# Wide-head attention with three-pass products, unrolled, in an eight-layer kernel on one NeuronCore

## Chip, cores and metric

The kernel runs on one core of one Trainium2 chip. The metric is the device time of one execution in microseconds, from which a run's time is taken; lower is better. PE is the engine of the matrix products, DVE the vector engine, ACT the scalar engine, POOL the GpSimd engine, SP the engine that issues most transfers.

## What is computed

Eight layers, each `x = x + layer(layernorm(x))`, on x of 32 sequences of 64 rows with 128 features (2048 rows, in 16 tiles of 128). The third layer is the one that changes:

```python
def _L1_xattn_ref(x, context, ln_gamma, ln_beta, w_q, w_kv, w_out, b_out, gate):
    xn = _layernorm(x, ln_gamma, ln_beta)
    q = (xn @ w_q).reshape(B, SQ, NUM_HEADS, DIM_HEAD)      # 16 heads of 64
    kv = context @ w_kv
    k, v = jnp.split(kv, 2, axis=-1)
    scores = jnp.einsum('bqhd,bkhd->bhqk', q * SCALE, k)
    attn = jax.nn.softmax(scores, axis=-1)
    out = jnp.einsum('bhqk,bkhd->bqhd', attn, v).reshape(B, SQ, INNER)
    out = out @ w_out + b_out
    return out * jnp.tanh(gate[0])
```

Its input is normalised twice, once by the residual step and once inside. The layer before it, F0, is a feed-forward layer (128 to 512 to 128, gelu); beside it the kernel already chooses the experts of a later mixture layer (E2) from the context alone.

## The kernel before

**Order.** Every engine runs one list of instructions, layer by layer; semaphores tie the lists together. An engine that waits holds up all that is behind it in its list. `experts` (L1214) writes the lists of F0, `wide_head_attention` (L864) those of the attention, `build` (L2712) what lies around them.

**Attention, per tile of 128 rows (two sequences).** The work of tile t is spread over five steps; step n handles tile n's norms and keys, n-1's rows and queries, n-2's scores and values, n-3's probabilities, n-4's output (L1037 to L1061). Steps 7 to 14 are a loop (`pipeline`, L48), the others are written out. On PE, in the order of a step: `scores` (L980), `turn_x` (L958, the normalised rows turned through the identity), `turn_probs` (L994), `queries` (L966), `turn_out` (L1020), `keys` (L933), `weigh_values` (L1006), `project` (L1031), `values` (L943). Queries, keys, values and the projection are float32 products.

Queries, keys, values and the turned rows share two PSUM banks, J0 and J1 (banks 0 and 1): whoever writes one waits until ACT or DVE has copied what was in it. Scores have two banks of their own, the turned probabilities, turned output and projection share two, the weighed values two.

ACT copies the turned rows with gamma and beta (L1075), the turned probabilities (L1083), queries (L1091), the turned output (L1099) and keys (L1107) out of PSUM and takes the exponentials (L1112). DVE does both norms (`Norm`, L125; each waits for POOL's power, L150), the maxima, subtraction, sums and division of the softmax, the gate and residual, and copies the values (L1197). POOL copies a piece of the context per tile for the value products (L1124).

**F0.** Its first products are already in three passes: a float32 operand is split into a high part in the format fp32r and the float32 rest, also kept in fp32r, and high x high, high x low and low x high are added up in PSUM (`product`, L1429):

```python
pe.matmul(out, WH[:, p, ws], XH[:, cols], start=True, stop=False)
pe.matmul(out, WH[:, p, ws], XL[:, cols], start=False, stop=False)
return pe.matmul(out, WL[:, p, ws], XH[:, cols], start=False, stop=True)
```

PE's list there: logits of the choice of experts (L1811), the turned norms (L234), first products of row groups 0 and 1, rank products (L1860), second products of group 0 (L1452), first of 2, second of 1, table products, first of 3, and so on. The rank products wait for DVE's `choose` (L1825): `take_best` twice (L1816: maximum, compare L1819, multiply L1821, maximum, compare L1823), then L1841 to L1844. POOL's list: the powers of the norms, the low parts of the rows (`low_part`, L245), then `owners` (L1614), which waits for DVE's places. DVE adds the second products to X, a row group at a time (L1719).

## Time and profile before

| | us |
|---|---|
| median of 3 runs | 964.1 (961.65 to 967.59) |
| profiled execution, span from first to last instruction | 1010.8 |
| profiled execution, what lies around the span | not recorded |
| busy in the span: PE / DVE / ACT / POOL | 783.2 / 608.2 / 486.4 / 372.9 |
| wide-head attention on PE, from / to | 147.6 / 343.8 |

The profiled execution is longer than the runs; its rows are used for durations and differences. Times in rows are microseconds from the start of the span unless marked ns. A float32 product shows as two records on PE, a product in fp32r as one; a record lasts longer than the distance to the next, since matmuls are pipelined, so distances are read from starts. "PEclk" is the granted clock of PE as a share of 2.4 GHz.

### The profile page before, as it was taken

The page shows a single profiled execution, that of the slowest core. Times are in us where ns is not written, and L with a number is a line of the kernel's source. Part 1 is how long each engine was busy: PE and PEld are TensorE (multiplying, and loading weights), DVE is VectorE, ACT ScalarE, POOL GpSimd, SP SyncE. Part 2 cuts the span into 40 slices and gives each one's busy share as a digit, 9 for nine tenths or more (in the row PEclk, how much of TensorE's full clock was granted, in tenths as well). Part 3 has the DMA queues.
Part 4 walks back from the last instruction along what each step waited for, and adds up shares of the span by engine and source line. Part 5 has one row for each costly group of instructions (what it writes and reads, how often), then busy time and mean ns, then how long its engine had stood idle before and what let it go on. Part 6 is the DMA issues. An engine that isn't in the chain of part 4 may idle for free.

```text
span 1010.8 us, 24129 instructions
## 1 busy us (share of the span) xinstructions
PE 783.2 (77%) x8041; PEld 646.4 (64%) x8041; DVE 608.2 (60%) x1568; ACT 486.4 (48%) x984; POOL 372.9 (37%) x492
## 2 busy tenths in 40 slices
PE   6998899999999789996477775667677559969005
PEld 3766787888888679985476664667676526644005
DVE  3886747777777667767353224632222368867895
ACT  3886434555444344432154435334444357745753
POOL 5663421111111331111566653155556535550810
PEclk9999699999999979999699989579989769978557
DMA  6300000000000000033332213101111300000001
GB/s 187 96 0 1 1 1 3 2 3 0 0 0 3 1 11 19 21 102 103 95 100 88 64 41 105 42 19 43 40 37 45 85 23 3 0 1 1 0 0 42
DMA packets 49218, 36.06 MB, mean 36 GB/s; under 512 B 7665, under 2 KB 44978, under 8 KB 49138
## 3 DMA queue, kind: packets, MB, share of 16 engines
q1 hardware_dynamic: 43420, 24.45, 8.5%
q0 software_dynamic: 4992, 10.23, 3.6%
q8 instruction: 48, 0.79, 0.3%
q10 hardware_dynamic: 726, 0.33, 0.1%
q14 instruction: 32, 0.26, 0.1%
HBM read 26.73 MB, written 8.26 MB: 35 GB/s over the span
## 4 chain that ended last, share of the span: by engine, by line
PE 67%; DVE 9%; another core or an unknown queue 6%; issue 5%; ACT 5%; DMA 3%; DVEq 2%; POOL 2%; ACTq 1%; SPq 1%; POOLq 0%
PE psum L2118 9%; PE psum L1464 7%; PE psum L2143 4%; PE psum L1034 3%; PE psum L976 3%; PE psum L954 3%; PE psum L939 3%; PE psum L2442 2%; PE psum L1431 2%; PE psum L1432 2%; PE psum L1433 2%; PE psum L323 2%; PE psum L1016 2%; PE psum L663 2%
## 5 line engine op out<-in xcount | busy, mean ns | idle before, releaser
L2118 PE MATMUL psum<-E_XT,E_weights 128*128 128x128 f32 x780 | 114.3, 298 | 52.4 <-ACT E_XT L2198 27.7
L2118 PEld LDWEIGHTS psum<-E_XT,E_weights 128*128 128x128 f32 x780 | 103.0, 209 | 61.2 <-ACT E_XT L2198 30.8
L2266 POOL DMA_INDIRECT y_scratch<-E_y,route_place_of x78 | 78.8, 1010 | 83.2 <-DVE E_y L2321 37.8
L2258 POOL DMA_INDIRECT E_rows<-rows_scratch,route_token_of x78 | 76.4, 979 | 32.1 <-issue 25.5
L1723 DVE SCALAR_TENSOR_TENSOR X<-psum,E_gates,X 128x128 f32<-128x128 f32 x256 | 71.7, 344 | 26.5 <-PE psum L1464 26.4
L1464 PEld LDWEIGHTS psum<-E_w,E_h 128*128 128x128 f32 x512 | 69.4, 198 | 11.5 <-issue 3.5
L2221 ACT ACTIVATE E_h<-psum,cols 128x128 f32<-128x128 f32 x156 | 44.5, 368 | 66.4 <-issue 31.3
L1548 ACT ACTIVATE E_h<-psum,cols 128x512 f32<-128x512 f32 x64 | 43.8, 687 | 67.8 <-PE psum L1433 67.7
L1464 PE MATMUL psum<-E_w,E_h 128*128 128x128 f32 x512 | 70.4, 282 | 4.8 <-DVE X L1723 3.8
L2311 DVE TENSOR_TENSOR E_h<-E_sg,psum 128x384 f32<-128x384 f32 x39 | 21.6, 554 | 77.5 <-remote 26.8
L203 POOL TENSOR_TENSOR rstd<-vareps,nhalf 128x4 f32<-128x4 f32 x24 | 24.6, 1029 | 75.0 <-DVE vareps L197 74.9
L235 PE MATMUL psum<-ident,xn 128*128 128x128 f32 x80 | 20.0, 400 | 35.9 <-ACT xn L226 24.5
L2143 PE MATMUL psum<-L1w,E_h 128*128 x312 | 44.4, 288 | 0.5 <-DVE E_y L2323 0.5
L150 POOL TENSOR_TENSOR A_A_inner_rstd<-A_A_inner_vareps,nhalf 128x1 f32<-128x1 f32 x16 | 8.7, 543 | 95.5 <-DVE A_A_inner_vareps L144 95.5
L788 POOL TENSOR_TENSOR A_kexp<-E_first,hmask 128x512 f32<-128x512 f32 x32 | 32.7, 1042 | 30.0 <-PE psum L663 29.9
L2431 PE MATMUL psum<-ident,Q_amax_rows 128*1 128x128 f32 x5 | 1.7, 332 | 52.1 <-DVE Q_amax_rows L2539 51.4
L235 PEld LDWEIGHTS psum<-ident,xn 128*128 128x128 f32 x80 | 14.0, 210 | 43.5 <-issue 21.5
L2323 DVE TENSOR_TENSOR E_y<-psum,E2b2all 128x128 f32<-128x128 f32 x39 | 11.3, 290 | 49.6 <-PE psum L2143 27.9
L2143 PEld LDWEIGHTS psum<-L1w,E_h 128*128 128x128 f32 x312 | 40.4, 202 | 1.0 <-issue 0.7
L2114 PE MATMUL psum<-ident,E_rows 128*128 128x128 f32 x78 | 22.8, 293 | 22.3 <-DMA E_rows<-rows_scratch,route_token_of 22.3
L2204 ACT ACTIVATE E_weights<-E_first 128x768 f32 x39 | 32.9, 843 | 14.2 <-issue 13.9
L1075 ACT ACTIVATE A_xnT<-psum,cols 128x128 f32<-128x128 f32 x16 | 7.3, 457 | 65.3 <-PE psum L964 65.3
(346 smaller groups left out, 2160.2 us busy)
## 6 DMA issues: line engine op xcount, KB each, us to landing
routed_back<-y_scratch SPq DMA_DIRECT2D x16, 256.0 KB, 4.9
E_first<-in_L_xattn_W SPq DMA_DIRECT2D x1, 2048.0 KB, 8.6
L1w<-in_L_xattn_W SPq DMA_DIRECT2D x8, 256.0 KB, 4.7
rows_scratch<-xn SPq DMA_DIRECT2D x8, 256.0 KB, 2.3
E_w<-in_L_ffn_routed_w SPq DMA_DIRECT2D x28, 64.0 KB, 1.9
E_raw<-in_L_ffn_w_down SPq DMA_DIRECT2D x8, 176.0 KB
E_rows<-rows_scratch,route_token_of POOLq DMA_INDIRECT x78
y_scratch<-E_y,route_place_of POOLq DMA_INDIRECT x78
```

The costliest lines, as they stand in the source:

```text
L235: tr = pe.transpose(self.bank[:, i * P:(i + 1) * P], self.m.xn[:, g * GT + i, :], self.m.ident[:, :])
L788: ke = pool.tensor_tensor(kexp[:, p, b], kk.broadcast_to([P, HP, S]), m.hmask[:, :].rearrange("p (h o) -> p h o", o=1).broadcast_to([P, HP ...
L939: mm = pe.matmul((J1, J0)[j][:, c * P:(c + 1) * P], w["k"][:, cc * P:(cc + 1) * P], columns(m.ctxT, t, P), start=True, stop=True)
L1464: mm = pe.matmul(y_bank(e, g)[:, i * P:(i + 1) * P], h[:, g % 2, c, i * P:(i + 1) * P], w2[:, p, c, :], start=(c == 0 and i == 0), stop=(c ...
L1548: act.activation(h[:, g % 2, c, :], ring[(C * g + c) % 4], spec["func"], bias=spec["b1"][:, bass.ds(e * C + c, 1)]).then_inc(h_ready.sem, 1)
L1723: st = dve.scalar_tensor_tensor(out=m.X[:, t, :], in0=y_bank(e, g)[:, i * P:(i + 1) * P], scalar=gates[:, t, bass.ds(e, 1)], in1=m.X[:, t, :],
L2118: mm = pe.matmul(out[:, c * P:(c + 1) * P], WE[:, p, (k0 + c) * P:(k0 + c + 1) * P], XT[:, p, :], start=True, stop=True)
L2143: mm = pe.matmul(Y[p][:, 0:P], h[:, p, c, :], W2[:, bass.ds(e, 1), c, :].rearrange("p o d -> p (o d)"), start=c == 0, stop=c == C - 1)
L2204: act.activation(WE[:, i % 2, :], W1[:, bass.ds(e, 1), :].rearrange("p o f -> p (o f)"), ACT.Copy).then_inc(w_ready.sem, 1)
L2221: ac = act.activation(h[:, p, c, :], m.banks[2 + i % 3][:, c * P:(c + 1) * P], spec["func"], bias=spec["b1"][:, bass.ds(e * C + c, 1)])
L2258: pool.indirect_dma_start(out=xg[:, i % 4, :], out_offset=None, in_=rows[:, :], in_offset=bass.IndirectOffsetOnAxis(ap=disp.token_of[:, i: ...
L2266: pool.indirect_dma_start(out=yrows[:, :], in_=y[:, i % 3, :], in_offset=None, out_offset=bass.IndirectOffsetOnAxis(ap=disp.place_of[:, i: ...
```

## The change

- Queries, keys and values are computed in three passes in fp32r instead of float32. Weights: ACT makes the high parts of the three matrices before F0 (`wide_high`), POOL the low parts inside F0, ahead of `owners` (`low_parts`). Context: ACT copies four high pieces and POOL subtracts four low ones at the start of the attention. Rows: ACT copies the turned rows twice (high part, full), POOL subtracts.
- Queries and keys are computed for a pair of tiles (256 columns) and half of the heads at a time, one such half per step. Values are one bank per half of the heads' dimension order; DVE copies those of even heads, ACT those of odd heads, two copies of 64 partitions each.
- The work of a tile spreads over seven steps; all are written out, no loop is left.
- On PE `turn_x` stands behind `turn_probs`, then keys, turned output, queries.
- The norms of tiles 0 and 1 are done by DVE in F0, ahead of the last two additions to X; two pairs' keys and one pair's queries stand in the lists ahead of the wait for F0's end.

The diff, cut:

```diff
+    xH, xL = (m.split_rows[:, i, :].rearrange("p (r q) -> p r q", q=PW) for i in range(2))
+    CH, CL = m.split
+    WH, WL = m.wide_high, m.wide_low
...
+        def three(out, wk, cc, xs, start=True):
+            ws = slice(cc * P, (cc + 1) * P)
+            pe.matmul(out, WH[:, wk, ws], xs[0], start=True, stop=False)
+            pe.matmul(out, WH[:, wk, ws], xs[1], start=False, stop=False)
+            return pe.matmul(out, WL[:, wk, ws], xs[0], start=False, stop=True)
...
+        def keys(i, free):
+            pair, half = i // 2, i % 2
+            cols = slice(pair * PW, (pair + 1) * PW)
+            pe.wait_ge(*ctx_low(pair // 2 + 1))
             for j in range(2):
...
+                if free[j]:
+                    pe.wait_ge(*free[j])
+                for c in range(2):
+                    mm = three((J1, J0)[j][:, c * PW:(c + 1) * PW], 1, 4 * half + 2 * j + c, (CH[:, cols], CL[:, cols]))
                 mm.then_inc(k_ps.sem, 1)
...
+        def turn_x(t, free):
+            pe.wait_ge(*xn_ready(t + 1))
+            if free:
+                pe.wait_ge(*free)
+            pe.transpose(J0[:, 0:P], xn[:, t % 2, :], m.ident[:, :]).then_inc(xnT_ps.sem, 1)
+        def queries(i, free):
...
+            pe.wait_ge(*x_low(2 * pair + 2))
+            for j in range(2):
+                pe.wait_ge(*free[j])
+                for c in range(2):
+                    mm = three((J1, J0)[j][:, c * PW:(c + 1) * PW], 0, 4 * half + 2 * j + c, (xH[:, r, :], xL[:, r, :]))
+                mm.then_inc(q_ps.sem, 1)
...
+                if n <= NT + 1:
+                    pe.wait_ge(*q_ready(2 * (n - 2) + u + 1))
                 else:
...
+                    pe.wait_ge(*(v_even, v_odd)[u](t))
+                bank = (J1, J0)[u]
+                pe.matmul(bank, CH[:, cols], wv[0][:, :, u, :], start=True, stop=False)
+                pe.matmul(bank, CL[:, cols], wv[0][:, :, u, :], start=False, stop=False)
+                mm = pe.matmul(bank, CH[:, cols], wv[1][:, :, u, :], start=False, stop=True)
                 mm.then_inc(v_ps.sem, 1)
...
+        turn_x(0, None)
+        keys(0, (None, xnT_ready(1)))
+        turn_x(1, k_ready(2))
+        keys(1, (k_ready(1), xnT_ready(2)))
+        queries(0, (k_ready(3), k_ready(4)))
+        queries(1, (q_ready(1), q_ready(2)))
+        keys(2, (q_ready(3), q_ready(4)))
+        keys(3, (k_ready(5), k_ready(6)))
+        m.begin(pe, start)
         def step(n, p):
             q = 1 - p
...
+            if is_tile(n - 4):
+                scores(n - 4)
+            if is_tile(n - 5):
+                turn_probs(n - 5, q)
+            if n >= 3 and is_tile(n - 1):
+                turn_x(n - 1, v_odd(n - 4) if n >= 5 else xnT_ready(3) if n == 4 else k_ready(8))
+            if after(tag) and n == NT + 4:
+                pe.wait_ge(*v_odd(NT))
+                after(tag).turn(pe, 0)
+            if 5 <= n <= NT:
+                keys(n - 1, (v_even(n - 4), xnT_ready(n)))
+            if is_tile(n - 6):
+                turn_out(n - 6, p)
+            if n == 4:
+                queries(2, (k_ready(7), xnT_ready(4)))
+            elif 5 <= n <= NT:
+                queries(n - 2, (k_ready(2 * n - 1), k_ready(2 * n)))
+            elif n == NT + 1:
+                queries(n - 2, (v_even(n - 4), v_odd(n - 4)))
+            if is_tile(n - 5):
+                weigh_values(n - 5, q)
+            if after(tag) and n == NT + 5:
+                after(tag).turn(pe, 1)
+            if is_tile(n - 6):
+                project(n - 6, p)
+            if is_tile(n - 4):
+                values(n - 4, n)
...
+        for g in range(NG):
+            cols = slice(g * GW, (g + 1) * GW)
+            act.activation(CH[:, cols], m.ctxT[:, cols], ACT.Copy).then_inc(ctx_high.sem, 1)
+        def keys_kept(i):
+            pair, half = i // 2, i % 2
+            if pair >= 2:
+                act.wait_ge(*scores_ready(2 * pair - 2))
+            for j in range(2):
+                c = 4 * half + 2 * j
+                act.wait_ge(*k_ps(2 * i + j + 1))
+                act.activation(kT[pair % 2][:, c:c + 2, :].rearrange("p c k -> p (c k)"), (J1, J0)[j],
+                               ACT.Copy).then_inc(k_ready.sem, 1)
+        def rows_kept(t):
...
+            act.activation(xH[:, t // 2 % 2, t % 2 * P:(t % 2 + 1) * P], J0[:, 0:P], ACT.Identity, bias=w["beta"],
+                           scale=w["gamma"])
+            if t >= 2:
+                act.wait_ge(*x_low(t - 1))
+            act.activation(xnT[:, t % 2, :], J0[:, 0:P], ACT.Identity, bias=w["beta"],
+                           scale=w["gamma"]).then_inc(xnT_ready.sem, 1)
+        def queries_kept(i):
+            pair, half = i // 2, i % 2
+            if pair >= 2:
+                act.wait_ge(*scores_ready(2 * pair - 2))
+            for j in range(2):
+                c = 4 * half + 2 * j
+                act.wait_ge(*q_ps(2 * i + j + 1))
+                act.activation(qT[pair % 2][:, c:c + 2, :].rearrange("p c q -> p (c q)"), (J1, J0)[j],
+                               ACT.Copy).then_inc(q_ready.sem, 1)
...
+            if is_tile(n - 5):
+                t = n - 5
+                if t >= 2:
                     act.wait_ge(*o_ps(t - 1))
                 for half in range(2):
                     act.wait_ge(*probT_ps(2 * t + half + 1))
                     act.activation(probT[:, q, 4 * half:4 * half + 4, :].rearrange("p c q -> p (c q)"),
                                    pP[:, half, :], ACT.Copy).then_inc(probT_ready.sem, 1)
...
+            if n >= 3 and is_tile(n - 1):
+                rows_kept(n - 1)
+            if 5 <= n <= NT:
+                keys_kept(n - 1)
+            if is_tile(n - 6):
+                t = n - 6
+                if t >= 2:
                     act.wait_ge(*out_ps(t - 1))
                 for j in range(2):
                     act.wait_ge(*oT_ps(2 * t + j + 1))
                     act.activation(oT[:, p, 4 * j:4 * j + 4, :].rearrange("p c q -> p (c q)"), pP[:, j, :],
                                    ACT.Copy).then_inc(oT_ready.sem, 1)
...
+            if n >= 4 and is_tile(n - 2):
+                queries_kept(n - 2)
+            if is_tile(n - 4):
+                act.wait_ge(*sub_ready(n - 3))
                 pr = prob[:, p].rearrange("p h k -> p (h k)")
                 act.activation(pr, pr, ACT.Exp, scale=scale).then_inc(prob_ready.sem, 1)
...
+                act.wait_ge(*v_ps(2 * n - 6))
+                if n >= 6:
+                    act.wait_ge(*o_ps(n - 5))
+                for b in range(2):
+                    cp = act.activation(v[S:P, p, b].rearrange("p c d -> p (c d)"), J0[b * S:(b + 1) * S, :], ACT.Copy)
+                cp.then_inc(v_odd.sem, 1)
...
+        for t in range(2):
+            outer.rstd(pool, t, t, x1_ready)
+            inner.rstd(pool, t, t, xn_ready)
+        for g in range(NG):
+            cols = slice(g * GW, (g + 1) * GW)
+            pool.wait_ge(*ctx_high(g + 1))
+            pool.tensor_tensor(CL[:, cols], m.ctxT[:, cols], CH[:, cols], ALU.subtract).then_inc(ctx_low.sem, 1)
...
+            pool.tensor_tensor(xL[:, t // 2 % 2, at], xnT[:, t % 2, :], xH[:, t // 2 % 2, at],
+                               ALU.subtract).then_inc(x_low.sem, 1)
+        low_part(0)
+        low_part(1)
         m.begin(pool, start)
...
+    def early_rows(dve, t):
+        outer.stats(dve, tile_of(m.X, t), t, t)
+        outer.apply(dve, x1[:, t, :], tile_of(m.X, t), t, t).then_inc(x1_ready.sem, 1)
+        dve.wait_ge(*x1_ready(t + 1))
+        inner.stats(dve, x1[:, t, :], t, t)
+        inner.apply(dve, xn[:, t, :], x1[:, t, :], t, t).then_inc(xn_ready.sem, 1)
...
+                dve.wait_ge(*v_ps(2 * t + 1))
                 for b in range(2):
...
+                    cp = dve.tensor_copy(v[0:S, p, b].rearrange("p c d -> p (c d)"), J1[b * S:(b + 1) * S, :])
+                cp.then_inc(v_even.sem, 1)
...
+            spec["pool_between"](pool)
             for j in range(NCH):
                 beside.owners(pool, j)
...
+                if beside and g >= 2:
+                    dve.wait_ge(*combined(1))
+                    m.early_rows(dve, g - 2)
                 dve.wait_ge(*y_ps(u + 1))
...
+        def low_parts(pool):
+            for i, k in enumerate((1, 0, 2)):
+                pool.wait_ge(wide_high_ready, i + 1)
+                pool.tensor_tensor(m.wide_low[:, k, :], wide[:, k, :], m.wide_high[:, k, :], ALU.subtract
+                                   ).then_inc(wide_low_ready, 1)
...
+            for k in (1, 0, 2):
+                act.activation(m.wide_high[:, k, :], wide[:, k, :], ACT.Copy).then_inc(wide_high_ready, 1)
             for L in layers[1:]:
                 L.scalar(act)
```

## Rows read from the trace of the kernel before

**Rows 1.** Windows: us, length, busy PE, PEld, DVE, ACT, POOL, PEclk, DMA.

```profile
240.00:270.00 30.00, 30.00 (x539) 24.65 (x529) 22.58 (x47) 13.25 (x24) 2.83 (x7) 1.00 0.00 0
147.60:343.80 196.20, 189.53 (x3226) 159.24 (x3227) 148.87 (x318) 95.08 (x164) 27.74 (x54) 1.00 0.01 2
```

**Rows 2.** Chain that ended last, one tile of the attention: start us, us, what.

```profile
232.68 1.09 PE psum L990 x64
234.03 0.87 PE psum L1001 x8
234.90 1.89 PE psum L976 x16
236.79 0.87 PE psum L1027 x8
237.66 1.79 PE psum L939 x16
239.45 1.09 PE psum L1016 x64
240.54 1.98 PE psum L1034 x16
242.53 1.87 PE psum L954 x8
244.39 1.09 PE psum L990 x64
```

**Rows 3.** Chain that ended last, in F0: one fp32r pass of 512 columns, 16 of 40.

```profile
123.27 0.23 PE psum L1433
...
134.08 1.70 PE psum L1930 x16
```

**Rows 4.** Timeline of the attention: start us, us, engine, line, operation [idle before].

```profile
245.41 0.33 PE L964 MATMUL psum<-ident,A_xn 128*128 128x128 f32 x1
...
245.58 1.04 PE L1001 MATMUL psum<-ident,A_prob 128*128 128x128 f32 x8
...
245.86 0.46 ACT L1075 ACTIVATE A_xnT<-psum,cols 128x128 f32<-128x128 f32 x1 [4.83 <-PE psum L964]
...
246.22 1.08 ACT L1083 ACTIVATE A_probT<-psum 128x512 f32<-128x512 f32 x2
...
246.45 2.04 PE L976 MATMUL psum<-A_xnT,L1w 128*128 128x128 f32 x16
```

**Rows 5.** Timeline of F0.

```profile
108.78 0.60 ACT L242 ACTIVATE F_XH<-psum 128x512 fp32r<-128x512 f32 x1 [8.10 <-PE psum L235]
...
114.65 1.28 POOL L249 TENSOR_TENSOR F_XL<-XNT,F_XH 128x512 fp32r<-128x512 f32 x1 [1.09 <-ACT XNT L243]
...
115.09 0.98 DVE L1819 TENSOR_TENSOR route_work<-route_logits,route_best 128x128 f32<-128x128 f32 x1
...
117.00 1.27 POOL L249 TENSOR_TENSOR F_XL<-XNT,F_XH 128x512 fp32r<-128x512 f32 x1 [1.08 <-ACT XNT L243]
...
118.78 0.29 DVE L1819 TENSOR_TENSOR route_work<-route_at,route_best 128x128 f32<-128x128 f32 x1
...
120.96 0.29 DVE L1844 TENSOR_TENSOR route_ahead<-route_upto,route_both 128x128 f32<-128x128 f32 x1
...
123.34 0.38 PE L1865 MATMUL psum<-route_both,earlier 128*128 128x128 f32 x2
...
147.62 0.69 DVE L1719 TENSOR_TENSOR X<-X,psum 128x512 f32<-128x512 f32 x1 [4.67 <-PE psum L1464]
```

**Rows 6.** Timeline of the layer behind the attention.

```profile
356.69 5.38 POOL L1607 TENSOR_SCALAR E_b2sel<-L1b2rep,tmask 128x128 f32<-128x128 f32 x8
...
358.72 0.39 DVE L1638 TENSOR_TENSOR E_work<-E_work,E_row 128x224 f32<-128x224 f32 x1
```

**Rows 7.** Windows behind a pause of PE, columns as in rows 1.

```profile
597.34:601.29 3.95, 0.01 (x1) 0.00 (x0) 0.72 (x2) 0.27 (x1) 1.95 (x2) 1.00 0.34 49
601.70:605.10 3.40, 3.40 (x18) 3.40 (x17) 1.01 (x3) 1.60 (x6) 1.95 (x2) 0.50 0.07 24
```

More of the change, by code:

```diff
@@ L919, in wide_head_attention, with steps, is_tile @@
     L.done = x_done(NT)
[L920 to L927 removed]
+    END = NT + 7
+    first_products_done = m.split_free
+    after = m.stats_after.get
+    def steps(step):
+        for n in range(2, END):
+            step(n, n % 2)
+    def is_tile(t):
+        return 0 <= t < NT
     def tensor(pe):
[L930 removed]
         pe.wait_ge(*m.dispatch.owner_ready(1))
[L933 to L983 removed]
@@ L984, in scores @@
+        def scores(t):
+            a, r = t % 2, t // 2 % 2
+            pe.wait_ge(*q_ready(4 * (t // 2) + 4))
+            pe.wait_ge(*k_ready(4 * (t // 2) + 4))
+            if t >= 1:
                 pe.wait_ge(*sub_ready(t))
@@ new lines, in step @@
+            if after(tag) and n == NT + 5:
[4 more added lines that the diff above has]
+                values(n - 4, n)
+        steps(step)
+    def scalar(act):
+        for s, n in first_products_done:
+            act.wait_ge(s, n)
+        for g in range(NG):
[11 more added lines that the diff above has]
+        def rows_kept(t):
+            act.wait_ge(*xnT_ps(t + 1))
+            if t >= 4:
+                act.wait_ge(*q_ps(4 * (t // 2) - 4))
+            act.activation(xH[:, t // 2 % 2, t % 2 * P:(t % 2 + 1) * P], J0[:, 0:P], ACT.Identity, bias=w["beta"],
[5 more added lines that the diff above has]
+        def queries_kept(i):
+            pair, half = i // 2, i % 2
+            if pair >= 2:
[5 more added lines that the diff above has]
+                               ACT.Copy).then_inc(q_ready.sem, 1)
+        rows_kept(0)
+        keys_kept(0)
+        rows_kept(1)
+        keys_kept(1)
+        queries_kept(0)
+        queries_kept(1)
+        keys_kept(2)
+        keys_kept(3)
@@ new lines, in step, with low_part @@
+            if after(tag) and NT + 4 <= n < NT + 6:
+                after(tag).evacuate(act, n - NT - 4)
+        steps(step)
+    def gpsimd(pool):
+        for t in range(2):
[5 more added lines that the diff above has]
+            pool.tensor_tensor(CL[:, cols], m.ctxT[:, cols], CH[:, cols], ALU.subtract).then_inc(ctx_low.sem, 1)
+        def low_part(t):
+            at = slice(t % 2 * P, (t % 2 + 1) * P)
+            pool.wait_ge(*xnT_ready(t + 1))
+            pool.tensor_tensor(xL[:, t // 2 % 2, at], xnT[:, t % 2, :], xH[:, t // 2 % 2, at],
+                               ALU.subtract).then_inc(x_low.sem, 1)
+        low_part(0)
+        low_part(1)
@@ L1119, in gpsimd @@
         m.begin(pool, start)
-        def context(t, p):
-            if past(t, 2):
-                pool.wait_ge(*v_ps(2 * t - 2))
-            pool.tensor_copy(ctx1[:, p, :], columns(m.ctxT, t, P)).then_inc(ctx1_ready.sem, 1)
+        outer.rstd(pool, 2, 0, x1_ready)
         def step(n, p):
-            if live(n):
+            if is_tile(n):
                 inner.rstd(pool, n, p, xn_ready)
-            if live(n + 1):
+            if n >= 3 and is_tile(n - 1):
+                low_part(n - 1)
+            if is_tile(n + 1):
@@ L1130, in step @@
                 outer.rstd(pool, n + 1, 1 - p, x1_ready)
-            if live(n - 1):
-                context(n - 1, 1 - p)
-        outer.rstd(pool, 0, 0, x1_ready)
-        pipeline(pool, step, LO, HI, END)
-        if begun(NT):
+        steps(step)
+        if after(tag):
             for g in range(NG - 1):
-                follower().rstd(pool, g)
+                after(tag).rstd(pool, g)
             for g in range(2):
-                follower().low_part(pool, g)
-                follower().residual(pool, g)
+                after(tag).low_part(pool, g)
+                after(tag).residual(pool, g)
@@ L2787, in build @@
         b0["o"] = spread("L0bo", ins["L0_xattn_bo"], load_first)
+        with ExitStack() as early:
+            m.wide_low = early.enter_context(nc.sbuf_tensor("L1w_low", [P, 3, 1024], F32R))
         wide = sb("L1w", [P, 4, 1024])
```

221 lines of the change are left out of this document (65 added, 156 removed).

## Prediction

> **What bounds the kernel now.** I read the busy windows first. The wide-head attention fills the stretch from 147.6 to 343.8 us, 196.2 us, with PE busy for 189.5 of them at granted clock 1.00, the 2.4 GHz level; inside it PE is busy for all 30.00 us from 240 to 270, while DVE has 22.58 and ACT 13.25 [rows 1]. The chain of waits then says what PE does there: one tile lasts 244.39 - 232.68 = 11.71 us and every piece is PE's, end to end [rows 2]. In order: scores 1.09 (and 0.26 up to the next piece, in which the rows of the next tile are turned), probabilities turned 0.87, queries 1.89, output turned 0.87, keys 1.79, values weighed 1.09, projection 1.98, values 1.87. So a microsecond taken from PE in a tile shortens the tile by as much, until PE has to wait for something.
>
> **Sum against which time.** The durations come from a profiled execution with a span of 1010.8 us, 46.7 above the median of 964.1 us of the runs. What I find is a difference inside the span, and I subtract it from the median unchanged; the stage concerned waits on no DMA.
>
> **Products in three passes.** Queries and keys are now 12 passes of 256 columns per tile each (24 per pair of tiles), values 6 of 512. A pass over 512 columns in the same format takes 0.23 us, one over 40 takes 1.70/16 = 0.106 [rows 3]. For 256 no row exists: below, 0.106; above, the straight line between the two, 0.163. I take half of the 512-column pass, 0.115, because the long pass is the nearer in that it streams columns for most of its time. Then queries cost 12 x 0.115 = 1.38 instead of 1.89, keys 1.38 instead of 1.79, values 6 x 0.23 = 1.38 instead of 1.87: 1.41 us less per tile, 16 x 1.41 = 22.6 us of PE time.
>
> **The rows turned behind the probabilities.** This gives much of it back. In a step PE now does: probabilities turned, rows turned (bank 0), first half of the keys (bank 1), second half of the keys (bank 0). The second half waits until ACT has emptied bank 0, and ACT's list in that step begins with the two copies of the turned probabilities, then two copies of the rows (high part and full) where there was one. From the start of the turned probabilities: ACT's first copy starts at 0.64 (245.58 to 246.22), the two take 1.08, so the rows start at 1.72; the first row copy lets the next start 0.36 later (245.86 to 246.22), the second takes 0.46, done at 2.54; PE follows 0.13 later (246.32 to 246.45), at 2.67 [rows 4]. PE itself was ready at 0.87 + 0.17 + 6 x 0.115 = 1.73. It stands for 0.94 us, in each of the 12 steps that have keys: 11.3 us. Bounds: 0, if ACT could copy the rows first, which its order forbids; 1.1 with passes of 0.106, since PE then only waits longer. The new steady tile is 11.71 - 1.41 + 0.94 = 11.24 us.
>
> What else waits in the step is covered. The turned rows need the odd values copied by ACT: about 0.2 + 2 x 0.6 = 1.4 us after the values, against 1.96 of scores and probabilities; cover gone, 1.4 would stand there. The even values keep DVE's two copies; DVE needs 22.58/30 x 11.71 = 8.8 us per tile, below 11.24. ACT rises from 5.2 by two copies and a row copy (1.6) to 6.8. Unrolling takes away loop bookkeeping that the chain doesn't show; I cost it at nothing, bounds 0.1 us per tile either way.
>
> **Filling and draining.** Before: 196.2 - 16 x 11.71 = 8.8 us in which no tile advances. Now four key products and two query products stand ahead, on two banks that ACT empties between uses. A half lasts 0.69, its copy is seen by PE after about 0.2 (the 0.64 above less half of 0.87) + 0.6 + 0.13 = 0.93, a turned tile of rows after 0.17 + 0.2 + 0.82 + 0.13 less the half behind which it hides, 0.5. The first two key products cost 0.5 + 0.93 + 0.5, the next four calls 0.24 each (0.69 + 0.93 for a bank against 1.38 of work), the last copy 0.93: 3.8 us. In the step of the first scores the third pair's queries wait for two tiles' rows one after the other and POOL's low part: about 3.4. With 5 for the drain, 12.2 to 13 instead of 8.8: +4.0. Bounds 0 and +8.
>
> Attention: -22.6 + 11.3 + 4.0 = -7.3 us.
>
> **Work put into the layer before.** ACT's three high parts of the weights (128x1024 each, twice the 0.60 copy, about 3.3 together) fall into its 8.10 us of idleness before 108.78; the first norms of two tiles fall into DVE's waits ahead of its last two additions to X, the last 4.67 [rows 5]. Both nothing; without the cover 3.3 and 3.8.
>
> POOL's three low parts are another matter. They follow POOL's last subtraction, which ends at 118.27, and POOL's next work is far off, so POOL's own time is free. But POOL's subtraction holds up DVE: an operation of DVE on two SBUF operands that met one took 0.98 us and ended 0.14 after POOL, alone it took 0.29 [rows 5]. The three new ones run just while DVE picks the two best experts, the chain from 118.78 to 121.25 on which PE's rank products wait. PE came to these at 123.34, 2.1 us later [rows 5]. Each new subtraction has 1024 columns, at most twice 1.27: 2.5 us. In turn with DVE: POOL to 120.8, best-of compare 120.95, POOL to 123.45, next multiply 123.6, POOL to 126.1, next compare 126.25, and the half of the chain that is left, 1.2 us: 127.45. PE stands for 4.2 us instead of nothing. If POOL went through first, 118.3 + 7.5 + 2.5 = 128.3: 5.0. The floor is 0, if DVE isn't held.
>
> A pause of that length also costs clock: after PE's pause of 3.95 us from 597.34 the granted clock was 0.50, the 1.2 GHz level, for the next 3.4 us of full work [rows 7]: 1.7 us lost. The layer before: 4.2 + 1.7 = +5.9, bounds 0 and 7.
>
> The Trainium skill's page "SBUF — State Buffer", section "SBUF: two separate sides", has VectorE and GpSimd share one pair of ports as a lock held for a whole instruction, against VectorE operations with two SBUF inputs. By it the wait is certain and the sum is the one I make, 962.7. The trace agrees for subtractions, but not for every POOL operation that reads SBUF: while POOL's multiplies by a column ran, DVE's two-operand compare took its plain 0.39 us [rows 6]; by those rows the sum would be 956.8.
>
> **Sum:** -7.3 + 5.9 = -1.4 us; 964.1 - 1.4 = 962.7 us.
>
> **Rivals.**
> *The low parts hold nobody up.* For it: rows 6. Against: the slowed compare in rows 5, same kind of POOL operation. Only the attention counts: 964.1 - 7.3 = 956.8 us. Chance 0.20.
> *The second half of the keys doesn't wait.* If ACT's copies overlap more than the rows show, the 11.3 us stay gained: 962.7 - 11.3 = 951.4. Against: four copies in a row on one engine. Chance 0.13.
> *The 256-column pass costs more than half the long one* (the slower side). Loading 128 columns of weights may set the pace, as it seems to with 40 columns at 0.106. 24 passes x 16 tiles less the 72 hidden in the wait are 312; each 0.01 us costs 3.1 us. From 0.12 on the kernel is slower than before; at 0.163 it is 962.7 + 312 x 0.048 = 977.7. Against: 512 columns at 0.23 leave little for the load. Chance 0.13.
> *The early keys don't come early,* because the low parts of the context on POOL come late: then the filling costs its bound, +4, 966.7. I keep it within the forecast's range.
>
> **How the numbers follow.** Forecast 0.54, its own range 958 to 968. One per cent, 9.6 us, is about what a measurement of this kernel can tell from no change. Faster by more: most of the second rival (0.12), a tail of the first (0.05) and of the forecast (0.02): 0.19. Slower by more: most of the pass rival (0.09) and a tail (0.02): 0.11. Within: 0.70. The range 950 to 972 takes in the first two rivals and the cheaper half of the third.
>
> **What would show it.** In the profile after: steady scores 11.1 to 11.4 us apart, with 0.9 us of idleness in the middle of the keys released by ACT's second row copy; 256-column passes at 0.115; DVE's compares stretched to over 2 us beside POOL's low parts, PE idle some 4 us ahead of the rank products, clock 0.50 after it; first scores about 12.5 us after the last product of the layer before. The forecast is wrong if the keys run without a gap, if the rank products start at 123.3 as before, or if a pass takes 0.13 or more.

## The result and the profile after

The changed kernel takes 966.8 us (median of 15 runs) against 961.8 us for the kernel before in the same measurement. The two medians lie 5.0 us apart; the ratio taken over all runs is smaller, 1.0034, interval 1.0019 to 1.0049, which is 3.3 us slower. The forecast was 1.4 us faster. A second measurement, beside the experiments, gave 1.0015 (0.9997 to 1.0034); the two intervals overlap.

The profiled execution after has a span of 965.1 us. The one before had 1010.8, but that difference lies behind the stretch compared here, in the later mixture layers, which the change does not touch. So I compare one stretch of the two traces: from F0's first product to the router's products behind the attention. It lasts from 115.45 to 344.08 before, 228.63 us, and from 115.31 to 346.97 after, 231.66 us: 3.03 more, close to the 3.3 of the ratio. It splits like this. F0 ends where its last product ends: before at 147.6 as in [rows 1] (the attention's first PE instruction starts at 148.36, after a wait of 0.78 us for DVE), after at 152.49, where the attention's first PE instruction follows at once. A step is counted from one tile's scores to the next tile's.

| stretch | before | after | difference |
|---|---|---|---|
| F0, from its first product to the end of its last | 32.15 | 37.18 | +5.03 |
| to the first scores | 9.28 | 12.76 | +3.48 |
| first scores to third scores | 16.55 | 18.61 | +2.06 |
| third scores to fourteenth (11 steps) | 129.42 | 124.70 | -4.72 |
| fourteenth scores to the router's products | 41.23 | 38.41 | -2.82 |

The busy windows of the kernel after, over the same marks (columns as in rows 1; the third window is the first of the two first steps alone):

```profile
115.30:152.50 37.20, 33.81 (x217) 30.88 (x215) 29.74 (x56) 16.53 (x26) 16.98 (x14) 0.89 0.00 1
152.50:165.25 12.75, 11.08 (x78) 9.48 (x76) 6.00 (x26) 9.06 (x17) 6.79 (x10) 1.00 0.00 1
165.25:174.98 9.73, 6.81 (x84) 5.51 (x84) 5.43 (x13) 3.75 (x7) 2.46 (x5) 0.65 0.01 3
183.86:308.56 124.70, 117.30 (x2103) 106.19 (x2102) 95.30 (x187) 78.86 (x143) 15.34 (x30) 1.00 0.01 3
308.56:346.97 38.41, 33.95 (x644) 29.97 (x643) 31.05 (x66) 20.59 (x35) 6.84 (x7) 1.00 0.01 2
```

PE, which stands for 0.87 of the 129.42 us of the steady stretch before, now stands for 7.40 of 124.70; and in the step of the first scores, 9.73 us, it is busy for 6.81 of them at a mean granted clock of 0.65.

**F0.** POOL's three low parts and DVE's choice of the second expert, in the timeline of the kernel after:

```profile
118.09 7.20 POOL L2944 TENSOR_TENSOR L1w_low<-L1w,L1w_high 128x1024 fp32r<-128x1024 f32 x3
...
118.31 0.28 DVE L1898 TENSOR_REDUCE route_best<-route_at 128x16 f32<-128x128 f32 x1
118.64 2.04 DVE L1899 TENSOR_TENSOR route_work<-route_at,route_best 128x128 f32<-128x128 f32 x1
120.71 2.38 DVE L1901 TENSOR_TENSOR route_work<-route_work,rev 128x128 f32<-128x128 f32 x1
123.12 0.29 DVE L1902 TENSOR_REDUCE route_rowmax<-route_work 128x16 f32<-128x128 f32 x1
123.44 2.00 DVE L1903 TENSOR_TENSOR route_second<-route_work,route_rowmax 128x128 f32<-128x128 f32 x1
...
126.71 0.49 PE L1945 MATMUL psum<-route_both,earlier 128*128 128x128 f32 x2 [3.39 <-DVE route_ahead L1924]
```

The compare that took 0.29 [rows 5] takes 2.04, and the two operations behind it 2.38 and 2.00: each ends when a low part ends. PE reaches the rank products at 126.71 instead of 123.34. From 127.06 to 130.48 the granted clock is 0.50. Six further traces have the same F0 (e0, e2, e3, e4, e9 and e10 below): the rank products come 11.39 to 11.41 us after the first product in each, PE stands for 3.46 to 4.46 us ahead of them, and F0 takes 37.17 to 38.18 us. A difference of less than 1 us in F0 between two traces therefore says little.

**A steady tile.** The chain of waits after, from one tile's scores to the next (rows to hold against [rows 2]):

```profile
240.59 1.09 PE psum L996 x64
241.68 0.60 PE psum L1007 x4
...
242.36 0.40 ACT A_probT L1142
...
242.85 0.59 ACT A_probT L1142
243.45 0.12 ACT A_xnT_split L1107
...
243.67 0.48 ACT A_xnT L1111
...
244.20 0.39 PE psum L940
244.58 0.12 PE psum L941
...
245.17 0.87 PE psum L1034 x8
246.05 0.12 PE psum L940
...
247.46 1.09 PE psum L1023 x64
248.55 1.98 PE psum L1041 x16
250.53 0.23 PE psum L980
...
251.93 0.20 PE psum L996
```

251.93 - 240.59 = 11.34 us. The chain leaves PE after the first half of the turned probabilities, runs through ACT's two copies of probabilities and two of rows, and comes back with the second half of the keys (L940 at 244.20). The timeline shows the gap: the first half's last pass starts at 243.24, and the second half at 244.20.

```profile
243.24 0.28 PE L942 MATMUL psum<-E_XH,L1w_low 128*128 128x256 f32 x1
244.20 0.39 PE L940 MATMUL psum<-E_XH,L1w_high 128*128 128x256 f32 x1 [0.68 <-ACT A_xnT L1111]
```

Less one pass of 0.12 that is 0.84 us. The product groups are as short as forecast: queries 246.05 to 247.46, 1.41; values 250.53 to 251.93, 1.40.

**The step of the first scores.** Timeline of PE and POOL there:

```profile
165.25 1.16 PE L996 MATMUL psum<-XNT,xn 64*64 64x64 f32 x64
166.40 0.30 PE L959 MATMUL psum<-ident,A_xn 128*128 128x128 f32 x1
169.61 0.58 PE L940 MATMUL psum<-A_xnT_split,L1w_high 128*128 128x256 f32 x1 [2.92 <-POOL A_xnT_split L1185]
...
172.34 0.63 PE L980 MATMUL psum<-L1w_high,E_XH 128*128 128x512 f32 x1
...
168.59 0.54 POOL L150 TENSOR_TENSOR A_A_inner_rstd<-A_A_inner_vareps,nhalf 128x1 f32<-128x1 f32 x1 [1.31 <-DVE A_A_inner_vareps L144]
169.11 0.45 POOL L1185 TENSOR_TENSOR A_xnT_split<-A_xnT,A_xnT_split 128x128 fp32r<-128x128 f32 x1
```

PE waits 2.92 us for POOL's low part of the fourth tile's rows; POOL makes it only after the inner norm of the fifth tile, for which it waits for DVE. The granted clock is 0.50 from 168.02 to 174.85, so that 12 passes of queries take 172.34 - 169.61 = 2.73 us (1.59 in the steady tile, also from start to start) and the values 174.98 - 172.34 = 2.64 (1.57).

**The end.** In the last three steps with scores there are no keys between the turned probabilities and the turned output; the two share PSUM banks. PE stands for 0.89 us in each of the three (at 311.63, 321.61 and 330.15). The kernel before, whose queries stand between the two, shows that wait in one step only, the last with scores. Timeline after, then before:

```profile
328.17 1.09 PE L1007 MATMUL psum<-ident,A_prob 128*128 128x128 f32 x8
330.15 1.06 PE L1034 MATMUL psum<-ident,A_on 128*128 128x128 f32 x8 [0.89 <-ACT A_probT L1142]
```

```profile
327.36 1.06 PE L1027 MATMUL psum<-ident,A_on 128*128 128x128 f32 x8 [0.89 <-ACT A_probT L1083]
```

### The profile page after: what moved, and what is told of

The parts are those of the page before. It is cut to its first block, busy times and chain, and to the rows that moved or that the text cites. A ratio compares the mean times of both kernels' runs of the same rounds, so it can differ in the third digit from the quotient of the medians.

```text
span 965.1 us, 23563 instructions
## 1 busy us (share of the span) xinstructions
PE 766.1 (79%) x7881; PEld 638.3 (66%) x7881; DVE 615.3 (64%) x1568; ACT 515.5 (53%) x1039; POOL 389.6 (40%) x499
## 4 chain that ended last, share of the span: by engine, by line
PE 60%; DVE 9%; POOL 9%; issue 8%; ACT 7%; DMA 5%; SPq 1%; ACTq 1%; DVEq 0%; POOLq 0%
PE psum L1540 7%; PE psum L2198 5%; PE psum L2223 4%; PE psum L1041 3%; POOL y_scratch L2346 3%; POOL E_rows L2338 3%; PE psum L2522 2%; DMA E_rows<-rows_scratch,route_token_of 2%; PE psum L323 2%; PE psum L1023 2%; PE psum L1507 2%; PE psum L1509 2%; ACT A_probT L1142 2%; PE psum L996 2%; PE psum L1508 2%
## 5 line engine op out<-in xcount | busy, mean ns | idle before, releaser
L2198 PE MATMUL psum<-E_XT,E_weights 128*128 128x128 f32 x780 | 104.2, 282 | 1.5 <-DVE E_XT L2376 0.8
L2198 PEld LDWEIGHTS psum<-E_XT,E_weights 128*128 128x128 f32 x780 | 97.2, 199 | 2.7 <-DVE E_XT L2376 1.5
L1166 ACT ACTIVATE A_v<-psum 64x512 f32<-64x512 f32 x32 | 18.9, 591 | 42.9 <-PE psum L982 42.7
L1655 POOL CAST E_WH<-E_w 128x128 fp32r<-128x128 f32 x16 | 4.6, 290 | 91.7 <-DMA E_w<-in_L_ffn_routed_w 72.5
```

The costliest lines, as they stand in the source:

```text
L2198: mm = pe.matmul(out[:, c * P:(c + 1) * P], WE[:, p, (k0 + c) * P:(k0 + c + 1) * P], XT[:, p, :], start=True, stop=True)
```

## The experiments

All start from the changed kernel. The stretches are read from each run's trace as in the table above; "first step" is from the first scores to the second, "whole" from F0's first product to the router's products.

| run | F0 | to first scores | first step | steady tile | whole | ratio to the kernel before |
|---|---|---|---|---|---|---|
| changed | 37.18 | 12.76 | 9.73 | 11.34 | 231.66 | 1.0034 (1.0019 to 1.0049) |
| changed, again (e0) | 37.79 | 12.75 | 9.78 | 11.34 | 232.34 | 1.0015 (0.9997 to 1.0034) |
| low parts apart (e1) | 32.04 | 12.76 | 8.90 | 11.34 | 225.67 | 0.9968 (0.9954 to 0.9982) |
| rows first (e2) | 37.20 | 12.75 | 9.78 | 10.73 | 224.93 | 0.9946 (0.9924 to 0.9967) |
| low part before norm (e3) | 37.62 | 12.75 | 7.41 | 11.34 | 229.76 | 0.9988 (0.9966 to 1.0010) |
| third pair early (e4) | 38.18 | 14.05 | 4.85 | 11.34 | 229.06 | 0.9980 (0.9958 to 1.0002) |
| e1, e2 and e4 (e5) | 31.66 | 14.05 | 4.84 | 10.73 | 215.58 | 0.9889 (0.9861 to 0.9917) |
| and the drain (e6) | 31.98 | 14.03 | 4.86 | 10.73 | 214.93 | 0.9867 (0.9848 to 0.9887) |
| one operand (e7) | 31.94 | 12.74 | 9.48 | 11.34 | 226.14 | one run, 960.6 us |
| norm order only (e8) | 35.13 | 12.75 | 8.89 | 11.34 | 228.75 | one run, 961.0 us |
| busy wait (e9) | 37.17 | 12.74 | 7.63 | 11.34 | 229.53 | 1.0008 (0.9989 to 1.0026) |
| fourth pass (e10) | 37.20 | 14.35 | 9.86 | 12.53 | 249.27 | one run, 979.8 us |

The ratios differ by up to 0.0024 from what the whole stretch says, in either direction (e0: 3.71 us more than before would be 1.0038, the ratio is 1.0015; e5: 13.05 less would be 0.9865, the ratio is 0.9889); the rest of the kernel, with lower-clock stretches of its own, is in the ratio too. Where a part is at issue I go by the stretch.

> The changed kernel once more, beside the others on one chip. It stands to the kernel before as it did: 1.0019 to 1.0049. If it comes out nearer to 1, the runs with one edit owe as much of their gain to the chip.

It came out at 1.0015, somewhat nearer to 1, so up to 0.002 of the gains in ratio may be the chip's. Its steps, 9.78 and 11.34, are those of the first trace; F0, 37.79, is 0.6 longer.

### F0: the low parts' place, their operands, the norm's order

```diff
+        norm.rstd(pool, 3)
+        between = spec.get("pool_between")
+        for g in range(2 if begun else 0, NG):
+            if between and g < 3:
+                between(pool, g)
+            norm.low_part(pool, g)
...
-            spec["pool_between"](pool)
             for j in range(NCH):
```

> Against the changed kernel (966.8 us). Only where POOL makes the three low parts of the weights changes: one ahead of each of its first three low parts of the rows, around 108 to 117 us, instead of all three behind the last one. Theory that the subtractions hold up DVE's expert-choosing chain: DVE's compares of the second choice are back at 0.3 to 1.2 us each, PE comes to the rank products at 123.3 to 124.5 instead of 126.71, the stretch at granted clock 0.50 behind them is gone, the attention's first PE instruction is at 147.5 to 148.7 instead of 152.49: 4 to 5 us less, 962 to 963, ratio to the kernel before 1.000 to 1.001. Rival, that PE's late rank products have another cause (DVE's order, the clock): 966.8, ratio 1.0034 to 1.005.

F0 took 32.04 us, 5.1 less, with PE busy in all of it and no lower clock behind the rank products, which came 7.96 us after the first product instead of 11.40. The whole stretch is 6.0 shorter, more than expected: the other 0.8 are in the step of the first scores, where PE waits 2.92 us as before but the granted clock is 0.50 for only 3.4 us.

```profile
118.08:150.12 32.04, 32.04 (x216) 29.36 (x215) 25.73 (x56) 16.58 (x26) 12.06 (x12) 0.92 0.00 1
```

But the edit does two things: the low parts move, and POOL's last power of the norms moves ahead of its first low part of the rows. So two further runs. The first leaves the place as it was and puts a multiplication by a column where the subtraction was. It reads one large operand instead of two, and the low parts themselves are left out:

```diff
-                pool.tensor_tensor(m.wide_low[:, k, :], wide[:, k, :], m.wide_high[:, k, :], ALU.subtract
+                pool.tensor_scalar(m.wide_low[:, k, :], wide[:, k, :], tmask16[:, 0:1], None, ALU.mult
```

> The weights' three low parts are left out: in their place, in the same place of POOL's list, stand three multiplications by a column, 128x1024 each, one large SBUF operand instead of two. Theory that it is the second operand (two reads of SBUF) that holds up DVE, as the multiplications in the kernel before's trace did not: DVE's second-choice compares take 0.3 to 0.5 us, rank products 8 us after the first product, no stretch at granted clock 0.50 behind them. Rival, that any POOL instruction that works on SBUF for so long holds DVE: compares of 1.5 to 2.5 us, rank products 11.4 us after the first product, as in the changed kernel.

Timeline of that run, the same operations of DVE beside POOL's multiplications (the third follows at once; the three take 9.22 us, longer than the subtractions' 7.20):

```profile
119.89 5.81 POOL L2944 TENSOR_SCALAR L1w_low<-L1w,tmask 128x1024 fp32r<-128x1024 f32 x2
...
120.41 0.77 DVE L1899 TENSOR_TENSOR route_work<-route_at,route_best 128x128 f32<-128x128 f32 x1
121.22 0.29 DVE L1901 TENSOR_TENSOR route_work<-route_work,rev 128x128 f32<-128x128 f32 x1
121.54 0.29 DVE L1902 TENSOR_REDUCE route_rowmax<-route_work 128x16 f32<-128x128 f32 x1
121.86 0.29 DVE L1903 TENSOR_TENSOR route_second<-route_work,route_rowmax 128x128 f32<-128x128 f32 x1
```

2.04, 2.38 and 2.00 us have become 0.77, 0.29 and 0.29, F0 takes 31.94 us, and nothing else was changed. It is POOL's two-operand subtraction that holds DVE; a longer instruction with one large operand holds it much less (one later operation, `route_ahead`, took 1.02 instead of 0.29). The edit changes the operation together with the number of operands, so that the second operand is the cause, and not the subtraction as such, is not shown.

The second does the norm's order alone:

```diff
-        if not begun:
-            norm.low_part(pool, 0)
         norm.rstd(pool, 3)
-        for g in range(2 if begun else 1, NG):
+        for g in range(2 if begun else 0, NG):
             norm.low_part(pool, g)
```

> Control for the run with the low parts apart, which also put POOL's last rstd ahead of its first low part of the rows: only that is done here, the weights' low parts stay behind the others. Theory (the place of the low parts did it): rank products 11.4 us after the layer's first product, as in the changed kernel. Rival (the earlier norm did it): about 8.

Here the rival was right about the rank products: they came 7.83 us after the first product. The earlier power lets DVE finish its norms and its choice by 116.89, before the low parts start at 117.98. F0 still took 35.13 us, because the hold now falls on what DVE does next:

```profile
123.93 0.94 DVE L1955 TENSOR_SCALAR route_ntile<-route_ntile 128x8 f32<-128x8 f32 x1
124.90 2.29 DVE L1956 TENSOR_TENSOR_SCAN route_ntile<-ones,route_ntile 128x8 f32<-128x8 f32 x1
...
134.60 1.07 PE L2008 MATMUL psum<-route_A,route_B 128*128 128x40 f32 x8 [0.96 <-POOL route_A L2000]
```

A scan over 8 columns takes 2.29 us (0.17 in the kernel after), the places come late, and PE stands for 0.96 us ahead of the table products, with the granted clock at 0.50 from 136.95 to 140.36. So of e1's 5.1 us the earlier norm alone gives 37.18 - 35.13 = 2.05, and with it in place the low parts' new place gives 35.13 - 32.04 = 3.1. These are single traces; F0 of the changed kernel alone differs by up to 1.0 us between traces.

### The steady tile: rows first

PE's list, then ACT's:

```diff
+            if n >= 3 and is_tile(n - 1):
+                turn_x(n - 1, v_odd(n - 4) if n >= 5 else xnT_ready(3) if n == 4 else k_ready(8))
             if is_tile(n - 5):
                 turn_probs(n - 5, q)
-            if n >= 3 and is_tile(n - 1):
-                turn_x(n - 1, v_odd(n - 4) if n >= 5 else xnT_ready(3) if n == 4 else k_ready(8))
```

```diff
+            if n >= 3 and is_tile(n - 1):
+                rows_kept(n - 1)
             if is_tile(n - 5):
...
-            if n >= 3 and is_tile(n - 1):
-                rows_kept(n - 1)
```

> Against the changed kernel (966.8 us). Rows are turned ahead of the probabilities, and ACT copies them ahead of the probabilities. Theory that the second half of the keys stands for ACT's row copies, 0.93 us in each of 12 steps: the gap in the keys is gone, PE waits 0.15 to 0.3 for the odd values ahead of the turned rows instead, the steady tile falls from 11.34 to 10.6 to 10.75, 12 x 0.6 to 0.75 = 7 to 9 us less: 958 to 960, ratio 0.996 to 0.998. Rival, that the wait for the odd values or the now later copies of the probabilities takes as much as the gap gave: tile 11.2 to 11.4, 965 to 967, ratio 1.002 to 1.004.

The tile fell to 10.73 us. The gap in the keys is gone, and PE waits 0.28 us for the odd values instead; the timeline of that run:

```profile
261.20 0.30 PE L959 MATMUL psum<-ident,A_xn 128*128 128x128 f32 x1 [0.28 <-ACT A_v L1166]
261.34 1.05 PE L1007 MATMUL psum<-ident,A_prob 128*128 128x128 f32 x8
...
263.65 1.03 PE L1034 MATMUL psum<-ident,A_on 128*128 128x128 f32 x8
```

From the turned probabilities to the turned output it is 2.31 us (261.34 to 263.65) where it was 3.40 (241.61 to 245.01, in the timeline of the changed kernel). The whole stretch is 6.7 us shorter, a little less than the 7 to 9 expected: 6.4 in the eleven steady steps and 0.4 in the second step.

The opposite probe adds work:

```diff
-            return pe.matmul(out, WL[:, wk, ws], xs[0], start=False, stop=True)
+            pe.matmul(out, WL[:, wk, ws], xs[0], start=False, stop=False)
+            return pe.matmul(out, WL[:, wk, ws], xs[1], start=False, stop=True)
```

(and the same in the values)

> The changed kernel with a fourth pass in each product of queries, keys and values (low part by low part): 4 passes of 256 columns more in queries, 4 in keys, 2 of 512 in values. By 0.117 and 0.235 a pass, with the two in the first half of the keys hidden in the wait for ACT's copies: 6 x 0.117 + 2 x 0.235 = 1.17 us more, a steady tile of 12.5 us with the gap in the keys down from 0.93 to 0.70; the last product of the attention some 18 us later. Rival, that PE isn't the bound or that the wait grows with the work: tile under 12.2, or 12.75 and more with the gap as it was.

The tile is 12.53 us. Six passes of 0.117 and two of 0.235 add 1.17, 1.19 were measured; the two passes in the first half of the keys cost nothing. The gap, read as above, shrank from 244.20 - 243.24 - 0.12 = 0.84 to 251.05 - 250.33 - 0.12 = 0.60, by just those two passes:

```profile
250.33 0.28 PE L943 MATMUL psum<-E_XL,L1w_low 128*128 128x256 f32 x1
251.05 0.39 PE L940 MATMUL psum<-E_XH,L1w_high 128*128 128x256 f32 x1 [0.44 <-ACT A_xnT L1113]
```

### The step of the first scores

```diff
+            if n == 4:
+                low_part(n - 1)
             if is_tile(n):
                 inner.rstd(pool, n, p, xn_ready)
-            if n >= 3 and is_tile(n - 1):
+            if (n == 3 or n >= 5) and is_tile(n - 1):
                 low_part(n - 1)
```

> Against the changed kernel (966.8 us). In the step of the first scores POOL makes the low part of the fourth tile's rows ahead of the inner norm of the fifth tile, instead of behind it; nothing else. Theory that the order on POOL holds up the third pair's queries: they start at 168.1 to 168.3 instead of 169.61, 1.4 us less, and as much as 2.2 more where PE's shorter pause keeps the granted clock at 1.00: 963.2 to 965.4, ratio 1.0015 to 1.0037. Rival, that ACT's copies or DVE's norm set the time of the queries: they start at 169.6, 966.8.

The step took 7.41 us, 2.3 less. The queries started 2.87 us after the first scores instead of 4.36, the 1.5 us that the theory said: the order on POOL was holding them up. The clock did not stay at 1.00, though; it was 0.50 for 3.4 us (168.97 to 172.39) instead of 6.8, which gives the other 0.8. The whole stretch is 1.9 shorter, with F0 0.4 longer.

The next run has the same order on POOL, and turns the third tile's rows between the early keys, the fourth's ahead of the first scores:

```diff
         keys(2, (q_ready(3), q_ready(4)))
-        keys(3, (k_ready(5), k_ready(6)))
+        turn_x(2, k_ready(6))
+        keys(3, (k_ready(5), xnT_ready(3)))
...
+            if n == 3:
+                turn_x(3, k_ready(8))
```

(and the same order of copies on ACT)

> Against the changed kernel (966.8 us). As the run with the low part ahead of the norm, and besides the rows of the third tile are turned and copied between the early keys of the third pair, those of the fourth ahead of the first scores. Theory that the lateness of the rows makes the step of the first scores long: the third pair's queries start at 166.4 to 167 instead of 169.61, 2.6 to 3.2 us less, and the granted clock stays at 1.00 through that step, 2.2 us more: from first scores to second scores 5 to 5.5 us instead of 9.73 if all goes well, and 961.5 to 963, ratio 0.9997 to 1.001. Rival, that the clock falls all the same, since it fell before the queries' wait had ended: 963.6 to 964.2, ratio 1.002. Rival, that the time comes back in the next step: no change.

The step took 4.85 us. The stretch to the first scores grew by 1.3, which the expectation had left out, so together 18.90 instead of 22.49. PE's wait and the windows of the step (columns as in rows 1):

```profile
173.82 0.38 PE L940 MATMUL psum<-A_xnT_split,L1w_high 128*128 128x256 f32 x1 [0.42 <-POOL A_xnT_split L1191]
```

```profile
172.23:177.08 4.85, 4.43 (x84) 3.48 (x83) 3.54 (x9) 2.95 (x5) 0.95 (x2) 1.00 0.01 3
```

The granted clock is 1.00 throughout. Whether that is because the pause is shorter could still be chance, so the next run keeps the pause and fills it:

```diff
             if n == 4:
+                pe.wait_ge(*k_ready(7))
+                for i in range(8):
+                    three(J1[:, i % 2 * PW:(i % 2 + 1) * PW], 1, 0, (CH[:, 0:PW], CL[:, 0:PW]))
                 queries(2, (k_ready(7), xnT_ready(4)))
```

> The changed kernel with 24 more passes of 256 columns on PE ahead of the third pair's queries, 24 x 0.117 = 2.8 us of work whose result is written over, in the time in which PE waits for the rows. Nothing else moves. Theory that 2.2 us of the step of the first scores are the lower clock alone: the granted clock stays at 1.00 through the step, queries take 1.4 to 1.6 us and values 1.5 to 1.6 as in the steady tiles, and the step from first to second scores is 7.4 to 7.7 us instead of 9.73 in spite of the added work; 2 us less in all. Rival, that the queries and values of that step are slow for another reason, or that the added work is not hidden: 9.5 to 10.5 us.

With 24 useless passes the step is 2.1 us shorter, 7.63 instead of 9.73, and its clock is 1.00, although the queries start as late as before, 4.38 us after the first scores (4.36 in the changed kernel; columns as in rows 1):

```profile
163.37:171.00 7.63, 7.53 (x108) 6.42 (x107) 4.95 (x13) 3.76 (x7) 2.47 (x5) 1.00 0.01 3
```

So 2.1 of the 9.73 us are the lower clock and nothing else. The price is not the same in every trace: with a wait of 2.9 us each, the step took 9.78 us in e0 and e2, 9.48 in e7, but 8.90 and 8.89 in e1 and e8, where the clock was 0.50 for 3.4 us instead of 6.8. Against 7.63 that is 1.3 to 2.2 us.

### All together, and the end

> The three edits that each helped, together: the weights' low parts apart, rows turned and copied ahead of the probabilities, the third pair's rows early. Theory that they act on three stretches that don't overlap: against the changed kernel 5.1 us less in the layer before, 12 x 0.61 = 7.3 in the steady tiles, 3.6 in the first steps, 16.0 together: from the first product of the layer before to the router products behind the attention 231.66 - 16.0 = 215.7 us, some 948 to 951 in all, ratio to the kernel before 0.986 to 0.989. Rival, that they share what they gain (PE waiting for the context's low parts or for the first norms where the layer before ends earlier): 10 to 13 less, ratio 0.989 to 0.992.

The whole stretch took 215.58 us, 16.1 less than the changed kernel's: the three parts add up. The run takes 951.9 us, ratio 0.9889.

```diff
+            if n >= NT + 2 and is_tile(n - 4):
+                values(n - 4, n)
             if after(tag) and n == NT + 4:
...
-            if is_tile(n - 4):
+            if n < NT + 2 and is_tile(n - 4):
                 values(n - 4, n)
```

> As the run with all three edits, and besides in the last two steps that have scores the values' products stand ahead of the turned output instead of at the step's end. Theory that PE's two waits of 0.89 us for ACT's copies of the probabilities, which the keys cover in the steady steps, come from nothing but the missing work: they are gone, 1.8 us less than the run with all three, the last scores 7.6 to 7.7 us after those before instead of 8.53. Rival, that the values now wait 0.3 to 0.5 each for the copies of those before and the copies come late for the products that weigh them: 0 to 0.8 less.

Scores to scores fell from 8.53 to 7.45 us, a little more than the theory said, but the step behind gained nothing: PE now reaches the last turned probabilities before DVE has read the projection from the same bank. The timeline of that run:

```profile
322.64 1.06 PE L1007 MATMUL psum<-ident,A_prob 128*128 128x128 f32 x8 [1.38 <-DVE A_tmp L1267]
```

From the fourteenth scores to the router's products it is 37.50 us instead of 38.41, so 0.91 of the 1.8 us are left; the whole stretch shows 0.65 because F0 came out 0.32 longer. The first of the three waits, at the fourteenth scores, stays. It is the fastest version of this study, 951.7 us and 0.9867 of the kernel before; its lead over the run without the last edit is within the intervals.

## Why the prediction was wrong

**The step that failed** is "Filling and draining", in the sum as +4.0 us with bounds 0 and +8. The attention was forecast at 7.3 us less and came out at 3.48 + 2.06 - 4.72 - 2.82 = -2.0; 5.3 us are missing. With the products' -22.6 and the gaps' +11.3 as they stand in the sum, that leaves +9.3 for filling and draining, or about +8.2 without what belongs to the steady tile: twice the forecast, at its upper bound. Where it went:

- The clock in the step of the first scores, 2.1 (busy wait run). The scores, the turned rows, the queries and the values of that step come to 1.09 + 0.26 + 1.38 + 1.38 = 4.1 by the prediction's prices, and with its wait of 3.4 to 7.5; the busy wait run shows 7.63. So the step was sized rightly, but I priced a pause's clock only in F0, where [rows 7] stood, and not here.
- The three waits of 0.89 us near the end instead of the one before, 1.8 more. I let ACT's copies of the probabilities stay hidden ("What else waits in the step is covered") although the keys that hide them are gone from those steps. The kernel before already showed the price, in its one step without keys and queries there (327.36). The drain run supports it: with the values put in between, two of the waits go, and 0.91 us are gained.
- The steady tile, 11.34 instead of 11.24: 1.1 over 11 steps.
- The rest, 0.3 to 0.4, lies in the start (12.76 instead of 12.5) and the first step. The 5 us for the drain were put in as one lump, so I can't say term by term what else changed there.

**The passes** were right: 0.115 forecast, 0.117 measured, queries 1.41 for 1.38, values 1.40 for 1.38. The rival with dearer passes is out.

**The gap in the keys** was right, and was the reason why three shorter products gain so little: 0.94 forecast, 0.84 measured. What made the tile 0.1 longer lies behind the gap: by the chain the second half of the keys takes 0.97 us (244.20 to 245.17) where I had 6 x 0.115 = 0.69, because the first pass after the wait counts 0.39 there and the others 0.12 (0.22 and 0.12 from start to start). Against that, the half starts 2.52 us after the turned probabilities rather than 2.67, and I had counted the turned rows as 0.26 in the tile and as 0.17 ahead of the gap, 0.09 too much. Turning rows and probabilities round takes the gap out (rows first), so the rival in which the keys don't wait was wrong for this order of the lists, and right for the other.

**F0** was right in mechanism and 0.9 too dear in this trace: +5.9 forecast, +5.03 measured; PE stood for 3.39 us rather than 4.2, and the clock's share is mostly in the second products behind it, 5.14 us where the later ones take 3.73 to 3.82. In the six other traces with the same F0 it is 5.0 to 6.0, so the forecast lies within what traces of this list show. The one-operand run answers the rival in which the low parts hold nobody: it would have been nearly right for a multiplication, as [rows 6] hinted, and was wrong for the subtraction, as [rows 5] said. By the lock that the Trainium skill's page "SBUF — State Buffer", section "SBUF: two separate sides", describes, any POOL operation that reads SBUF would hold DVE's two-operand ones; here the trace agrees for subtractions (2.00 to 2.38 us) and not for multiplications by a column (0.29 for two of the three, 0.77 for the first).

**The sum:** 5.3 too little in the attention less 0.9 too much in F0 is 4.4, which is the distance from -1.4 to the +3.03 of the two traces. A forecast this near to zero had its sign decided by a term whose own bounds were 8 us apart.

## What to carry to other kernels

A wait of PE can be paid twice, once as idleness and once in the clock of the work behind it: weigh the second price at every wait of a forecast, and not only at the one for which a row lies at hand. Here the waits of 3.39 us in F0 and 2.92 us in the step of the first scores came with 3.4 and 6.8 us at granted clock 0.50, and one of 1.43 us (low part before norm) with 3.4. It does not always happen: in the kernel before PE stands for 3.1 of the 9.28 us ahead of the first scores, 1.76 of them in one wait, and the clock stays at 1.00. When an engine's work is hidden by other work, go through the first and last steps by themselves, because there the cover is missing. An instruction put into an idle engine's list is not free if it reads two operands from SBUF beside DVE's chain; moving it to where DVE has slack gained about 3 us here.

## What the runs showed of the hardware that I had not expected

POOL's subtraction also held DVE operations that read one large operand from SBUF. In the run with the low parts apart, four norm multiplications that take 1.11 us without a subtraction beside them took 7.11, while POOL made low parts of weights and rows:

```profile
110.15 7.11 DVE L211 TENSOR_SCALAR xn<-X,meanvar,rstd 128x128 f32<-128x128 f32 x4 [0.41 <-POOL rstd L203]
```

A reduction that started 0.22 us into a low part took its plain 0.28 us (118.31 in the kernel after), so not every DVE read of SBUF is held. And the hold seems to work the other way too: in the run with the norm order only, DVE's addition over 128x2048 (2.28 us, from 117.98) ran through, and POOL's three low parts beside it took 9.17 us instead of 7.20.
